# Token sums of the experts' inputs: which operand stands still on TensorE, and gate logits by VectorE

## The reference, cut to what matters

```python
x = _layernorm(h, axis=-1)                                  # [32, 153, 192]
scores = jax.nn.softmax(jnp.mean(x, axis=1) @ Wg.T, axis=-1)  # Wg is [3, 192]
_, idx = jax.lax.top_k(scores, 1)
h1 = gelu(x @ W1[e] + b1[e]); y = h1 @ W2[e] + b2[e]        # e = the chosen expert
h = h + y * scores[chosen]
```

## Time and profile before

| | |
|---|---|
| median of 3 runs | 1062.55 us (1058.76 to 1064.7) |
| the profiled execution's own time | 1063.51 us |
| its span, first to last instruction | 1061.7 us |
| mean granted TensorE clock | 0.812 |
| busy share of the span | DVE 83%, PE 69%, ACT 67%, PEld 48%, POOL 16% |
| `ffn_inputs` in the span | about 820 to 890.4 us |
| `experts`, first matmul | 895.98 us |

### The profile page before, as it was taken

The page is one execution under the profiler, slowest core; times in us unless marked ns, Lnnn a source line. Parts: engine busy times, 40 slices in busy tenths (PEclk is TensorE's granted clock), DMA queues, the critical chain, the costliest instruction groups (busy, mean ns, idle before and its releaser), DMA issues. The chain is left out here.

```text
span 1061.7 us, 22846 instructions
## 1 busy us (share of the span) xinstructions
PE 737.1 (69%) x6039; PEld 511.8 (48%) x6040; DVE 883.0 (83%) x2418; ACT 712.6 (67%) x1376; POOL 172.3 (16%) x274
## 2 busy tenths in 40 slices
PE   3773386747888366666666667667534796999997
PEld 3562244424555234333333334343223685899896
DVE  5888987888888899999999999999968732676766
ACT  0344364957888698988899898998841563545443
POOL 5851400017554000000000000000006420000000
PEclk9986598988999687888877777887756555999999
DMA  7000000001111111111111111110040003455452
GB/s 250 3 2 0 0 1 1 0 0 38 37 37 35 32 28 27 26 23 24 24 24 23 23 23 28 24 24 21 12 156 3 10 1 113 145 191 197 158 203 87
DMA packets 84368, 54.59 MB, mean 51 GB/s; under 512 B 53832, under 2 KB 83304, under 8 KB 84072
## 3 DMA queue, kind: packets, MB, share of 16 engines
q1 hardware_dynamic: 83304, 53.97, 16.7%
q0 software_dynamic: 1024, 0.13, 0.2%
HBM read 11.77 MB, written 3.76 MB: 15 GB/s over the span
## 5 line engine op out<-in xcount | busy, mean ns | idle before, releaser
L1358 DVE SCALAR_TENSOR_TENSOR expo<-expo,con,pow 128x153 f32<-128x153 f32 x480 | 146.0, 376 | 0.7 <-ACT expo L1267 0.7
L1141 PE MATMUL at_rem<-word,ident_half 128*128 128x459 f16 x160 | 66.6, 416 | 102.3 <-ACT expo L1267 101.2
L1267 ACT ACTIVATE expo<-at_rem,con 128x459 f32<-128x459 f32 x160 | 95.3, 639 | 14.8 <-PE at_rem L1142 14.1
L953 DVE TENSOR_REDUCE rs_ends<-rs_banks 128x770 f32 (+1 forms) x96 | 91.3, 959 | 14.7 <-PE rs_banks L924 13.1
L873 ACT ACTIVATE rs_banks<-rs_banks 128x770 f32<-128x770 f32 x96 | 76.3, 798 | 25.5 <-PE rs_banks L916 24.1
L1141 PEld LDWEIGHTS at_rem<-word,ident_half 128*128 128x128 f16 x160 | 15.7, 98 | 152.5 <-ACT expo L1267 147.8
L1401 DVE CUSTOM_DVE_ANT_0 weight_top<-weight_top,line 128x2448 uint16<-128x2448 uint16 x64 | 86.2, 1346 | 2.1 <-ACT line L1259 2.1
L1223 ACT ACTIVATE word<-at_banks 128x459 uint8<-128x459 f32 x160 | 80.8, 560 | 10.3 <-PE at_banks L779 10.2
L1259 ACT ACTIVATE line<-weight_top 128x1224 f32<-128x1224 f32 x64 | 74.0, 1158 | 15.0 <-DVE weight_top L1386 14.7
L774 PE MATMUL at_banks<-pick,row_top 128*128 128x459 bf16 x160 | 73.1, 457 | 10.9 <-ACT word L1223 4.1
L1915 ACT ACTIVATE qk<-e_p,b1s 128x153 f32<-128x153 f32 x192 | 58.8, 391 | 29.9 <-PE e_p L1876 28.6
(11 more groups left out here) (393 smaller groups left out, 2158.8 us busy)
## 6 DMA issues: line engine op xcount, KB each, us to landing
qk<-vt SPq DMA_DIRECT2D x64, 384.0 KB, 3.0
rs_kb<-qk SPq DMA_DIRECT2D x128, 28.7 KB, 1.9
kb<-qk SPq DMA_DIRECT2D x128, 28.7 KB, 1.9
patches<-in_patches SPq DMA_DIRECT2D x4, 768.0 KB
vi<-vt SPq DMA_DIRECT2D x32, 96.0 KB, 2.0
out<-vi SPq DMA_DIRECT2D x32, 96.0 KB, 1.8
pj_w<-in_w SPq DMA_DIRECT2D x1, 2304.0 KB, 8.2
qb<-qk SPq DMA_DIRECT2D x128, 6.0 KB, 1.8
```

Of the source, the lines that this page charges most:

```text
L953: v.tensor_reduce(ends[:, :, n, 5 * b:5 * b + 5], banks[:, slot(u, b), :, 0:5 * W].rearrange("p i (t n) -> p i t n", n=W), AX, ALU.max).th ...
L1141: pe.matmul(out, identh[:, :], bank(word, b).bitcast(F16), start=True, stop=False)
L1267: act.activation(bank(ex, b), rem[:, (u + b) % 2, 0:3 * N], ACT.Square, scale=2.0 ** 24, bias=c(5)).then_inc(sq_done, 1)
L1358: ins = v.scalar_tensor_tensor(ex[:, t, :], ex[:, t, :], c(7), pw[:, t, :].bitcast(BF16), ALU.add, ALU.mult, accum_out=tot[:, t:t + 1])
```

## The change

Three things are changed, all in `ffn_inputs` and in the layout of its two small inputs.

In `token_sums` the operands change places. The stationary operand is now a window of 32 columns of `each`, zero but for one column of ones (or four columns with ones for one image strip each), and the normalized tile moves past it, all 192 channels in one matmul. The window is cut so that the ones stand in the column of the sequence, and all 40 matmuls add into one table, now with the 32 sequences on partitions and the channels along the row. There are 5 matmuls in a group in place of 10. `each` grows from 128 x 5 to 128 x 123.

The gate's logits are now made by DVE out of that table: for each expert one multiply of the table with a row of `wg` (copied to 32 partitions, 32 x 576 in place of 128 x 6), with 1/153 as the scalar and the sum over the row as second result. The scaling L1762, the matmuls L1677 and the hop from DVE to PE and back are left out; the maximum and the subtraction read `lg` in place of PSUM.

```diff
--- before.py
+++ after.py
@@ -1584,11 +1584,11 @@
         y16, xn = five(flat("vbd")[:, E * FT * C:E * FT * C + 10 * C].bitcast(I16)), five(flat("line")[:, 0:10 * C])
         stat, mv = sb("f_stat", [P, 5, 6]), sb("f_mv", [P, G, 5, 2])
         var, rstd, shift, power = (sb("f_" + x, [P, G, 5]) for x in ("var", "rstd", "shift", "power"))
-        minus, ones, each, wg, sums = sb("f_minus", [P, P], BF16), sb("f_ones", [32, P]), sb("f_each", [P, 5]), sb("f_wg", [P, 2, E]), sb("f_sums", [P, 2, B])
+        minus, ones, each, wg, products = sb("f_minus", [P, P], BF16), sb("f_ones", [32, P]), sb("f_each", [P, 2 * B - 1 + 2 * B - 4]), sb("f_wg", [32, E, C]), sb("f_products", [32, C])
         lg, mx, tot, inv, hit, pick, spread = (sb("f_" + x, s) for x, s in (("lg", [32, E]), ("mx", [32, 1]), ("tot", [32, 1]), ("inv", [32, 1]),
                                                                             ("hit", [32, E]), ("pick", [32, E + 1]), ("spread", [32, 5, 32])))
         ptx, pim = k.ps("f_ptx", [P, 2, 2, 512], F32, st), k.ps("f_pim", [P, 2, 512], F32, st)
-        psum, pg = k.ps("f_psum", [P, 512], F32, st)[:, 0:2 * B].rearrange("p (t b) -> p t b", t=2), k.ps("f_pg", [P, 512], F32, st)
+        psum, pg = k.ps("f_psum", [P, 512], F32, st)[0:B, 0:C], k.ps("f_pg", [P, 512], F32, st)
         loaded, y_int, h_ok, made, hi_ok, lo_ps, lo_ok, summed, eready, edone, gready, gps, negated, xn2_ok = (
             k.sem("f_" + x) for x in ("loaded", "y_int", "h_ok", "made", "hi_ok", "lo_ps", "lo_ok", "summed", "eready", "edone", "gready", "gps", "negated", "xn2_ok"))
 
@@ -1647,11 +1647,9 @@
                 def token_sums(g):
 
                     u = g % 2
-                    for kt in range(2):
-                        for w in range(4):
-                            pe.matmul(psum[0:CK[kt], kt, 4 * g + w:4 * g + w + 1], xn[:, u, w, channels(kt)], each[:, 0:1],
-                                      start=(g == 0 and kt == 0 and w == 0), stop=False, skip_group_check=True)
-                        mm = pe.matmul(psum[0:CK[kt], kt, 4 * g:4 * g + 4], xn[:, u, 4, channels(kt)], each[:, 1:5], start=False, stop=True, skip_group_check=True)
+                    for w in range(5):
+                        at = B - 1 - 4 * g - w if w < 4 else 2 * B - 1 + B - 4 - 4 * g
+                        mm = pe.matmul(psum, each[:, at:at + B], xn[:, u, w, :], start=(g == 0 and w == 0), stop=(g == G - 1 and w == 4))
                     mm.then_inc(summed, 1)
 
                 def low_parts(g):
@@ -1673,10 +1671,6 @@
                     if g + 1 < G:
                         token_sums(g + 1)
                 pe.wait_ge(gready, 1)
-                for kt in range(2):
-                    mm = pe.matmul(pg[0:32, 0:E], sums[0:CK[kt], kt, :], wg[0:CK[kt], kt, :], start=(kt == 0), stop=(kt == 1))
-                mm.then_inc(gps, 1)
-                pe.wait_ge(gready, 2)
                 pe.matmul(pg[:, 32:32 + 5 * 32], ones[:, :], spread[:, :, :].rearrange("p i b -> p (i b)"), start=True, stop=True).then_inc(gps, 1)
 
             @block.scalar
@@ -1758,12 +1752,10 @@
 
                 v.wait_ge(loaded, 64)
                 v.wait_ge(summed, G)
-                for kt in range(2):
-                    ins = v.tensor_scalar(sums[0:CK[kt], kt, :], psum[0:CK[kt], kt, :], 1.0 / N, None, ALU.mult)
-                ins.then_inc(gready, 1)
-                v.wait_ge(gps, 1)
-                link(v.tensor_reduce(mx[:, :], pg[0:32, 0:E], AX, ALU.max))
-                v.tensor_scalar(lg[:, :], pg[0:32, 0:E], mx[:, 0:1], None, ALU.subtract).then_inc(eready, 1)
+                for e in range(E):
+                    link(v.scalar_tensor_tensor(products[:, :], psum, 1.0 / N, wg[:, e, :], ALU.mult, ALU.mult, accum_out=lg[:, e:e + 1]))
+                link(v.tensor_reduce(mx[:, :], lg[:, :], AX, ALU.max))
+                v.tensor_scalar(lg[:, :], lg[:, :], mx[:, 0:1], None, ALU.subtract).then_inc(eready, 1)
                 v.wait_ge(edone, 1)
                 link(v.reciprocal(inv[:, :], tot[:, :]))
                 link(v.tensor_scalar(lg[:, :], lg[:, :], inv[:, 0:1], None, ALU.mult))
@@ -1779,7 +1771,7 @@
                     link(v.tensor_scalar(pick[:, e:e + 1], hit[:, 2:3], float(e), None, ALU.is_equal))
                     v.tensor_scalar(spread[:, 2 + e, :], ident[0:32, 0:32], pick[:, e:e + 1], None, ALU.mult)
                 v.tensor_scalar(spread[:, 1, :], ident[0:32, 0:32], mx[:, 0:1], None, ALU.mult).then_inc(gready, 1)
-                v.wait_ge(gps, 2)
+                v.wait_ge(gps, 1)
                 every = pg[:, 32:32 + 5 * 32].rearrange("p (i b) -> p i b", i=5)
                 link(v.tensor_copy(sel[:, :], every[:, 0, :]))
                 v.tensor_copy(m["chosen"][:, :, :], every[:, 2:5, :])
@@ -2084,13 +2076,11 @@
     r["w1"] = twice(f["L0_ffn_W1"].transpose(1, 0, 2)).reshape(2, P, E, FF).transpose(1, 0, 2, 3)
     r["b1"] = f["L0_ffn_b1"].reshape(E, FT, P).transpose(2, 0, 1)
     r["w2"] = f["L0_ffn_W2"].reshape(E, FT, P, C).transpose(2, 0, 1, 3)
-    wg = np.zeros((2 * P, E), np.float32)
-    wg[:C] = f["L0_ffn_Wg"].T
-    r["wg"] = wg.reshape(2, P, E).transpose(1, 0, 2)
-    each = np.zeros((P, 5), np.float32)
-    each[:, 0] = 1.0
+    r["wg"] = np.broadcast_to(f["L0_ffn_Wg"], (B, E, C))
+    each = np.zeros((P, 2 * B - 1 + 2 * B - 4), np.float32)
+    each[:, B - 1] = 1.0
     for j in range(4):
-        each[32 * j + ID:32 * j + 32, 1 + j] = 1.0
+        each[32 * j + ID:32 * j + 32, 2 * B - 1 + B - 4 + j] = 1.0
     r["each"] = each
     r["b2"] = np.broadcast_to(f["L0_ffn_b2"], (P, E, C))
     return {n: np.ascontiguousarray(a) for n, a in r.items()}
```

## The result

The changed kernel takes 1046.86 us (median of 4 runs, 1041.93 to 1049.09) against 1062.05 us before (4 runs); the ratio is 0.9852, 95% interval 0.9807 to 0.9897.

What follows compares the result with a forecast made beforehand. PE was taken to pace the block at the lower clock. Exponentials starting 13.2 us earlier, taken from 1063.51 us, gave 1050.3, or 1049.4 from the median; the forecast was 1050 us, range 1046.5 to 1057.5.

Steps and rivals of the forecast that it cites:

- What bound the block: From the first transpose to the gate, PE sets the pace with rounds of 6.88 us, 3.39 us of them sums.
- The clock: In the block, PE's clock rises from 0.50 to 1.00 some 3 to 6 us after the first transpose.
- Case C: Block's clock stays at 0.50, as only 32 of 128 columns hold weights or otherwise; 1.7 us gained, 1061 us; chance 0.16.
- The sums at the lower clock: In PE's token sums, 10 records of 0.32 us take 3.20 us a group in place of 3.39; 1.5 us gained.
- Case D: Clock stays at 0.50 and the sums' weight loads aren't hidden: 0.43 us a record, 7 us slower, 1070 us; chance 0.05.
- The round at the upper clock: PE's round in the block at clock 1.00 takes 3.55 us, under DVE's 4.96, with sums of 1.63 us.
- The pace: With PE fast, DVE sets the block's rounds at 4.96 us; it sees the last sums at 869.45, before at 883.04.
- my sum: The whole gain, 13.2 us: the gate's exponentials start at 871.9 in place of 885.07.
- The gate: DVE's multiplies up to the subtraction take 1.8 us, before 1.99; ACT's table load hides up to 0.65 us of it.
- Inputs: The larger `each` and `wg` load before PE's first use, hidden by some 4 us; otherwise under 1 us.

Runs made afterwards that it cites:

- e2: Kernel before the change, each sum moving a window of 32 columns in place of 1 or 4 past the same tile; ratio to before 0.9972.
- e3: Kernel before the change, each sum moving a window of 64 columns in place of 1 or 4 past the same tile; ratio to before 0.9824.
- e4: Kernel before the change, each sum moving a window of 128 columns in place of 1 or 4 past the same tile; ratio to before 0.986.
- e7: Changed kernel with the sums over only 2 of 192 channels after the first matmul, the rest left out; ratio to before 0.9862.
- e5: Changed kernel with one exponential of a constant at the head of ACT's list, so the table load comes early; ratio to before 0.9845.
- e1: The changed kernel again with no edit, for a second profile and more runs; ratio to before 0.9855.
- e6: Changed kernel with POOL making normalized tile 1 in ACT's place; ratio to before 0.9872.
- e9: Changed kernel with POOL's power replaced by a multiply, so all normalized values differ; ratio to before 0.9854.
- e10: Changed kernel with both POOL's power replaced by a multiply and tile 1 made by POOL in ACT's place; ratio to before 0.9823.

## Why the prediction came out as it did

- *What bound the block*: right. PE's round of 6.88 us went, and the waits for it with it.
- *The clock*: right, and e2 to e4 show it as the cause. It rose shortly before 829, over 3 us after the first transpose, where 3 to 6 were said, and stayed up through the gaps of all rounds, the longest 1.22 us, until the gate. Case C's reason, only 32 columns of weights in the array, fell: the clock was 1.00 with them. The Trainium skill (TensorE: Matmul & The Clock Gate, Part 4) says that transposes don't bring the full clock. The rise in the earlier trace rows speaks against that for float32, since in the 2.9 us from 55.41 to the rise at 58.3 all but the last 0.3 us were transposes, and e7, where the clock rose with transposes and 1.3 us of low parts in a round, doesn't support it either.
- *The sums at the lower clock*: right, 0.32 us a record forecast and 0.32 seen in e5 with 32 columns of weights. Case D's 0.43 us is not seen.
- *The round at the upper clock*: right for PE, 0.163 us a record forecast, (852.02 - 850.21) / 10 = 0.18 seen with the last one's end.
- *The pace*: this step failed, "DVE sets it ... shift 7 comes five rounds later, 837.00 + 5 x 4.96": it had the wrong engine for the steady rounds, and the round too long. I took 4.96 us from the earlier trace rows, which both follow a long power, as DVE's fixed round. The trace of before had short ones too, at 851.37 and 864.78, which I didn't look for. With short ones DVE's round is 4.13 us. ACT's I had put at 4.69 by adding the two stretches of the earlier trace rows; they overlap, and it is 4.48. The last shift came at 852.11, 27.0 us after the first transpose, and not 32.4; the exponentials at 863.45, 38.4 and not 42.5. From that shift on it took 11.3 us and not 10.1, for ACT was behind: its normalizing of group 7 began at 853.77, 1.66 us after the shift, where the forecast had it start at once. What remains, 4.1 us, is the whole of the difference between the 13.2 us of my sum and the 17.35 us of the block. In e1, with four long powers, the block gained 15.75, 2.6 over my sum; the medians differ by 15.2. So the time at the edge of the range comes from this term. Where exactly the time falls owes something to chance, as the long powers make the block of one profile 1.6 us longer than that of the other.
- *The gate*: 1.56 us to the logits where I had 1.8; hidden by the table load as forecast, 0.8 us of it (I had 0.65).
- *Inputs*: hidden. The first transpose comes 9.2 us after the block's first DMA in both kernels (829.37 - 820.14, 825.07 - 815.83).

## To carry to other kernels

When PE is busy all the time and its granted clock stays at 0.50, look at how many columns move in its matmuls: here those of one and four columns kept it busy with weight loads, and the clock was low for everything around them. Swapping the operands, or moving 64 or 128 columns of mostly zeros, brought it up, and 32 did not in the two executions profiled; then ask which engine's round is next. And when a round is read from a trace, look at all of its instances: an instruction of two lengths makes two rounds.

## What was not expected of the hardware

POOL's power of 128 x 5 values takes 1.19 or 2.09 us, by turns, in the same program with the same data; with a tile made by POOL after it (e6) it was 2.09 in seven of eight groups. The extra 0.9 us is not the power's own. With a multiply in its place (e9) the instruction takes 1.08 us in the first group and 0.20 in the others, and in e10 the extra time can move to POOL's next instruction. Here are two groups of e10, each with DVE's residual in it (the line of `Hres`):

```profile
831.66 0.20 POOL L1624 TENSOR_TENSOR f_rstd<-f_var,f_power 128x5 f32<-128x5 f32 x1
831.69 1.33 DVE L1732 SCALAR_TENSOR_TENSOR Hres<-vbd,qp,Hres 128x768 f32<-128x768 int16 x2
...
831.99 1.88 POOL L1628 TENSOR_SCALAR line<-Hres,f_mv,f_rstd 128x192 f32<-128x192 f32 x1
...
840.05 1.09 POOL L1624 TENSOR_TENSOR f_rstd<-f_var,f_power 128x5 f32<-128x5 f32 x1
840.08 1.33 DVE L1732 SCALAR_TENSOR_TENSOR Hres<-vbd,qp,Hres 128x768 f32<-128x768 int16 x2
...
841.25 1.26 POOL L1628 TENSOR_SCALAR line<-Hres,f_mv,f_rstd 128x192 f32<-128x192 f32 x1
```

In every group but the last, DVE's residual starts within 0.05 us of POOL's power or multiply. In the last group DVE has no residual left to do, and there the instruction is short in all 13 profiles; in the first group, where the two start within 0.01 us, it is long in all 13. So the long ones look like POOL waiting for DVE when the two start together, with small differences in time deciding which of POOL's instructions pays. This is read from the traces; no run moved DVE's residual away, so the cause is not shown.

The row sum of a multiply on VectorE costs a second entry of 0.07 us: 0.39 us from one 32 x 192 multiply to the next.
